# Keys in the heads' channels for two cross-attentions, quotients taken from PSUM, remainders by halves

## What is computed

```python
HEAD_DIM = DIM // NUM_HEADS          # 128 // 16 = 8
Q = (x @ Wq.T).reshape(B, xN, NUM_HEADS, HEAD_DIM)
KV = (z @ Wkv.T).reshape(B, zN, 2, NUM_HEADS, HEAD_DIM)
K = KV[:, :, 0]
V = KV[:, :, 1]
attn = jnp.einsum('bqhd,bkhd->bhqk', Q, K) * SCALE
attn = jax.nn.softmax(attn, axis=-1)
O = jnp.einsum('bhqk,bkhd->bqhd', attn, V).reshape(B, xN, DIM)
return O @ Wo.T
```

## Time and profile before

| | |
|---|---|
| runs | 4034.22, 4035.7, 4037.05 us, median 4035.7 us |
| profiled execution | 4029.83 us, span of the core 4028.0 us |
| busy share of the span | TensorE 94%, VectorE 78%, ScalarE 66%, GpSimd 63% |
| chain that ended last | TensorE 87%, VectorE 6%, GpSimd 2%, ScalarE 2% |
| granted TensorE clock, mean | 0.954 |

### The profile page before, as it was taken

The page is one execution under the profiler, slowest core; times in us unless marked ns, Lnnn a source line. Parts: engine busy times, 40 slices in busy tenths (PEclk is TensorE's granted clock), DMA queues, the critical chain, the costliest instruction groups (busy, mean ns, idle before and its releaser), DMA issues.

```text
span 4028.0 us, 110585 instructions
## 1 busy us (share of the span) xinstructions
PE 3794.2 (94%) x43467; PEld 2887.3 (72%) x43467; DVE 3136.7 (78%) x6499; ACT 2673.5 (66%) x5365; POOL 2545.3 (63%) x2457
## 2 busy tenths in 40 slices
PE   6999999989979999999799999996997899999987
PEld 4777777766647777777577777775665677777765
DVE  6999999858888888887688887886654788888864
ACT  4887887756647777777377777772542577777752
POOL 4888888759856766677466766664001476676761
PEclk8999999979989999999699999997998899999998
DMA  5333333125432221221122122110000212222100
GB/s 130 104 110 111 112 107 109 41 90 159 142 111 57 60 61 54 60 61 43 28 60 61 54 61 61 54 56 19 3 1 18 65 54 64 57 58 63 55 22 15
DMA packets 157328, 266.80 MB, mean 66 GB/s; under 512 B 26632, under 2 KB 97432, under 8 KB 155432
## 3 DMA queue, kind: packets, MB, share of 16 engines
q1 hardware_dynamic: 156360, 259.67, 22.6%
q10 hardware_dynamic: 448, 0.06, 0.0%
HBM read 165.10 MB, written 50.26 MB: 53 GB/s over the span
## 4 chain that ended last, share of the span: by engine, by line
PE 87%; DVE 6%; POOL 2%; ACT 2%; DMA 1%; issue 1%; SPq 1%; POOLq 0%; DVEq 0%; ACTq 0%
PE ps L186 83%; PE ps L665 1%; DVE xn L166 1%; POOL wst L545 1%; PE ps L242 1%; DVE wst L823 1%; PE ps L255 1%; PE ps L1639 1%; DMA big<-big 1%; PE ps L1161 0%; DVE st L151 0%; DVE wst L778 0%; DVE relu L775 0%; ACT wb L324 0%; PE ps L193 0%
## 5 line engine op out<-in xcount | busy, mean ns | idle before, releaser
L545 POOL TENSOR_TENSOR wst<-wst 125x384 bf16<-125x384 f32 (+1 forms) x1536 | 1432.2, 932 | 833.1 <-ACT wst L751 772.3
L751 ACT ACTIVATE wst<-ps 125x448 f32<-125x448 f32 x3072 | 1518.1, 553 | 568.3 <-PE ps L186 553.8
L186 PE MATMUL ps<-big,cx 128*125 128x448 bf16 (+1 forms) x6144 | 1427.4, 353 | 0.7 <-DMA big<-topT 0.7
L186 PEld LDWEIGHTS ps<-cx,wst 125*128 125x128 bf16 x23040 | 1113.6, 98 | 307.5 <-POOL wst L545 15.2
L823 DVE TENSOR_TENSOR wst<-wst 125x512 bf16<-125x512 f32 (+1 forms) x1536 | 1270.2, 827 | 56.7 <-ACT wst L751 56.5
L186 PE MATMUL ps<-cx,wst 125*128 125x65 bf16 (+2 forms) x23040 | 1202.4, 204 | 12.1 <-POOL wst L545 11.6
L186 PEld LDWEIGHTS ps<-big,cx 128*125 128x125 bf16 (+1 forms) x6144 | 834.5, 137 | 283.9 <-issue 1.8
L186 PE MATMUL ps<-cx,big 128*128 128x500 bf16 (+1 forms) x2688 | 709.8, 317 | 10.2 <-DVE big L1744 2.6
L778 DVE TENSOR_REDUCE wst<-ps 128x1 f32<-128x500 f32 x896 | 604.5, 675 | 136.3 <-PE ps L186 123.6
L775 DVE CUSTOM_DVE_ANT_0 wst<-ps,wst 128x500 bf16<-128x500 f32 x448 | 302.9, 676 | 195.0 <-PE ps L186 150.5
L775 DVE CUSTOM_DVE_ANT_0 relu<-ps,relu 128x500 bf16<-128x500 f32 x448 | 302.1, 674 | 149.7 <-PE ps L186 81.4
(11 more groups left out here) (250 smaller groups left out, 4213.2 us busy)
## 6 DMA issues: line engine op xcount, KB each, us to landing
big<-big SPq DMA_DIRECT2D x768, 56.0 KB, 2.7
cx<-ctxT SPq DMA_DIRECT2D x96, 375.0 KB, 3.5
cx<-ctxN SPq DMA_DIRECT2D x64, 377.9 KB
cx<-in_ctxN SPq DMA_DIRECT2D x64, 375.0 KB
cx<-ctxT SPq DMA_DIRECT2D x96, 187.5 KB, 3.8
ctxN<-cx SPq DMA_DIRECT2D x32, 377.9 KB
ynN<-cx SPq DMA_DIRECT2D x32, 377.9 KB
cx<-ynN SPq DMA_DIRECT2D x32, 377.9 KB
```

What stands on the lines that cost most here:

```text
L186: return t.matmul(o, l, r, start=start, stop=stop, skip_group_check=True)
L545: g.tensor_tensor(pl[r][0:KP, at:], pf[r][0:KP, at:], pf[r][0:KP, at:].bitcast(BF16)[:, 1::2], ALU.subtract).then_inc(s["plp"], 1)
L751: e.activation(pf[T % 3][0:KP, cols], bank(2 + n2 % 3, 448)[0:KP], ACT.Exp, scale=scale).then_inc(s["ev"], 1)
```

## The change

In stages 1 and 2 the keys are now projected on the chip into the heads' own channels (16 heads x 8 = 128 rows). Per batch three times two matmuls of 500 columns into bank 7 (`pe_keys`), ScalarE makes the high part `KH` (`act_keys`), VectorE the low part `KL` (`dve_keys`); both are stored to DRAM (`headk`) and loaded back in four groups of four heads, three times 32 rows (high, low, high) and a row of ones (`Ks`). The query is projected once for a pair of batches (three matmuls of 128 columns), stored to DRAM so that it lies block-diagonal there (`headq`), and loaded back as `Qm` (128 x 896, for the maxima) and `Qs` (97 x 896, for the scores). A score half is then two matmuls of 224 columns instead of two of 448. New loops `pe_head`, `act_head`, `dve_head`, `sp_head` hold the schedule of these two stages. The folding of query weights ahead of them falls away; stage 2's bias enters with the query.

In all four stages the values' 129-column matmul is split in 65 and 64, the accumulator has two buffers (`acc`), and a batch's end becomes: reciprocal and quotient on VectorE out of PSUM, rounding on ScalarE, remainder on GpSimd.

The remainder's border is 640, 448, 448, 512 for the four stages. In stages 1 and 2 VectorE's part now waits for the first exponential half alone, and GpSimd's part waits in addition until VectorE's of the same step is done (`s["pl"]`). Eight DMAs that clear `headq` are added at the program's start, ahead of the first context loads.

```diff
-JP = (5, 4, 4, 4)
+SPLIT = (640, 448, 448, 512)
...
+        acc = [bank(5 + i, 65 * NJ) for i in range(2)]
...
+        KH, KL = ([cTs[:, 1500 * v + 750 * i:1500 * v + 750 * i + 750].bitcast(BF16) for i in range(2)] for v in range(2))
+        Ks = [big[:, 3008 * i:3008 * i + 3008].bitcast(BF16).rearrange("p (g n) -> p g n", g=4) for i in range(2)]
+        Qm = [big[:, 6016 + 448 * i:6464 + 448 * i].bitcast(BF16) for i in range(2)]
+        Qs = [big[:, 6912 + 448 * i:7360 + 448 * i].bitcast(BF16) for i in range(3)]
+        kD = nc.dram_tensor("headk", [2, 2, 128, M], BF16).ap()
+        qD = nc.dram_tensor("headq", [4, 2, H * (8 * HQ + NQ)], BF16).ap()
...
+            if f in EARLY:
+                w.wait_ge(s["w"], (0, 224, 336)[f])
+                e.activation(wqh, wqs[:, 0:128], ACT.Copy).then_inc(s["f1a"], 1)
+                e.activation(wkh, wks, ACT.Copy).then_inc(s["f1a"], 1)
+            for j in () if f in EARLY else range(1 if f == 3 else 0, H // per, 2 if f == 3 else 1):
...
-                    r, at = (T - 1) % 3, 128 * JP[ci]
+                    r, at = (T - 1) % 3, SPLIT[ci]
                     w.wait_ge(s["ev"], evacuated(ci, T - 1) + 2)
+                    if ci in (1, 2):
+                        w.wait_ge(s["pl"], NT * ci + T)
                     g.tensor_tensor(pl[r][0:KP, at:], pf[r][0:KP, at:], pf[r][0:KP, at:].bitcast(BF16)[:, 1::2],
                                     ALU.subtract).then_inc(s["plp"], 1)
                     w.wait_ge(s["plp"], NT * ci + T)
-                if 0 <= (k := due(T, KT + 4)) < B - 1:
-                    u, kb = k % 2, B * ci + k
-                    r = raw[u][:, :, 0:C]
-                    w.wait_ge(s["fc"], 2 * (kb + 1))
-                    g.tensor_tensor(r, r, raw[u][:, :, C + 1:], ALU.add).then_inc(s["fp"], 1)
-                    w.wait_ge(s["fp"], 4 * kb + 1)
...
-                if 0 <= (k := due(T, KT + 8)) < B - 1:
-                    u, kb = k % 2, B * ci + k
-                    r = raw[u][:, :, 0:C]
...
-                    g.tensor_copy(O[:, k % HB, :, 0:C], r).then_inc(s["fp"], 1)
-                    w.wait_ge(s["fp"], 4 * kb + 3)
-                if 0 <= (k := due(T, KT + 10)) < B - 1:
-                    u, kb = k % 2, B * ci + k
-                    r = raw[u][:, :, 0:C]
-                    g.tensor_tensor(O[:, k % HB, :, C:], r, O[:, k % HB, :, 0:C], ALU.subtract).then_inc(s["fp"], 1)
-                    w.wait_ge(s["fp"], 4 * kb + 4)
+                if 0 <= (k := due(T, KT + 6)) < B - 1:
+                    kb = B * ci + k
+                    w.wait_ge(s["fp"], 2 * kb + 1)
+                    g.tensor_tensor(O[:, k % HB, :, C:], raw[k % 2], O[:, k % HB, :, 0:C], ALU.subtract).then_inc(s["fp"], 1)
+                    w.wait_ge(s["fp"], 2 * kb + 2)
+
+        def pe_values(t, w, ci, T):
+            k, i = divmod(T, KT)
+            r, kb = T % 3, B * ci + k
+            ph, o, of = pf[r][0:KP, :].bitcast(BF16)[:, 1::2], acc[k % 2], cnb[k % 3]
+            w.wait_ge(s["pl"], NT * ci + T + 1)
+            wait_values(w, ci, k)
+            if kb >= 2:
+                w.wait_ge(s["fc"], kb - 1)
+            for j in range(NJ):
+                if 128 * j == SPLIT[ci] or j == 3 and SPLIT[ci] == 448:
+                    w.wait_ge(s["plp"], NT * ci + T + 1)
+                cols, at = slice(128 * j, 128 * j + 128), 65 * j
+                mm(t, o[:, at:at + 65], ph[:, cols], of[:, i, 0:65], i == 0 and j == 0, False)
+                mm(t, o[:, at:at + 64], ph[:, cols], of[:, i, 65:129], False, False)
+                n = mm(t, o[:, at:at + 65], pl[r][0:KP, cols], of[:, i, 0:65], False, i == KT - 1)
+            n.then_inc(s["pv"], 1)
+
+        def dve_values(v, w, ci, k):
+            u, kb = k % 2, B * ci + k
+            o = acc[u].rearrange("p (j c) -> p j c", j=NJ)
+            w.wait_ge(s["pv"], KT * (kb + 1))
+            v.reciprocal(rden[u][:, :], o[:, :, C]).then_inc(s["rd"], 1)
+            if k >= 2:
+                w.wait_ge(s["fp"], 2 * (kb - 1))
+            w.wait_ge(s["rd"], kb + 1)
+            v.tensor_tensor(raw[u], o[:, :, 0:C], per_row(rden[u][:, :], C), ALU.mult).then_inc(s["fc"], 1)
+            if k == B - 1:
+                w.wait_ge(s["fp"], 2 * kb + 1)
+                v.tensor_tensor(O[:, k % HB, :, C:], raw[u], O[:, k % HB, :, 0:C], ALU.subtract).then_inc(s["fp"], 1)
+
+        def act_values(e, w, ci, k):
+            kb = B * ci + k
+            w.wait_ge(s["fc"], kb + 1)
+            w.wait_ge(s["fp"], 2 * kb)
+            if k >= HB:
+                w.wait_ge(s["otr"], kb - HB + 1)
+            e.activation(O[:, k % HB, :, 0:C], raw[k % 2], ACT.Copy).then_inc(s["fp"], 1)
...
+        KEY_SLOT = {21: (4, 0), 1: (2, 1), 4: (2, 2), 8: (3, 0), 12: (3, 1), 16: (3, 2)}
...
+        def sp_head(y, w, ci):
...
+            for T in range(-44, NT):
+                if (k := due(T, -44)) >= 0:
+                    i = k % 3
+                    if k >= 3:
+                        w.wait_ge(s["pm"], projected(ci, "keys", k - 3, 2))
+                    y.dma_start(cs[i], cT2[k]).then_inc(s[f"lT_{i}"], 16)
+                if (k := due(T, -18)) >= 0:
+                    u = k % 2
+                    w.wait_ge(s["pa"], projected(ci, "keys", k, 2))
+                    if k >= 2:
+                        wait_operands(w, ci, k - 2)
+                    y.dma_start(kD[u, 0], KH[u]).then_inc(s[f"stT_{u}"], 16)
+                    w.wait_ge(s["pd"], projected_low(ci, "keys", k, 2))
+                    y.dma_start(kD[u, 1], KL[u]).then_inc(s[f"stT_{u}"], 16)
+                if (m := 0 if T == -44 else (T + 23) // 24 if (T + 23) % 24 == 0 and T > 0 else NP) < NP:
...
+                    w.wait_ge(s["pa"], projected(ci, "query", m))
+                    for v, of in enumerate((qhb, qlb)):
+                        for r in range(2):
+                            y.dma_start(diagonal(qD[2 * (m % 2) + r, v]), of[m % 2][:, 64 * r:64 * r + NQ]).then_inc(s[f"qd_{m % 2}"], 16)
+                        w.wait_ge(s["pd"], projected_low(ci, "query", m))
+                if (k := 0 if T == -44 else due(T, -22) or -1) >= 0:
+                    wait_query_stored(w, ci, k // 2)
+                    if k >= 2:
+                        w.wait_ge(s["mxm"], products_to(b0 + k - 1, ORDER[0]))
+                    y.dma_start(Qm[k % 2], rows_of(qD[k % 4, 0])).then_inc(s[f"ql_{k % 2}"], 16)
+                if (k := due(T, -14)) >= 0:
+                    if k >= 2:
+                        wait_operands(w, ci, k - 2)
+                    if k >= 3:
...
+                    for n, v in enumerate((0, 0, 1)):
+                        y.dma_start(Qs[k % 3][32 * n:32 * n + 32, :].rearrange("r (g c) -> r g c", g=4),
+                                    grouped(qD[k % 4, v])).then_inc(s[f"lx_{k % 2}"], 16)
+                if (k := due(T, -11)) >= 0:
+                    u = k % 2
+                    wait_keys_stored(w, ci, k)
+                    if k >= 2:
+                        w.wait_ge(s["sc"], 2 * (t0 + KT * (k - 1)))
+                    for n, v in enumerate((0, 1, 0)):
+                        y.dma_start(Ks[u][32 * n:32 * n + 32, :, 0:M], by_group(kD[u, v])).then_inc(s[f"lx_{u}"], 16)
...
+                if (k := due(T, -3)) >= 0:
+                    w.wait_ge(s["ev"], (2 * NT + B) * ci + 2 * max(0, KT * k - 4) + k + 1)
+                    y.dma_start(Qs[k % 3][96:97, :], topT[k % 2][:, :]).then_inc(s[f"tops_{k % 2}"], 16)
+        def pe_keys(t, w, ci, k, c):
+            wait_keys(w, ci, k)
+            o, of = bank(keys_bank(k, c), 500), cs[k % 3][:, 500 * c:500 * c + 500]
+            mm(t, o, wkh, of, True, False)
+            mm(t, o, wkl, of, False, True).then_inc(s["pm"], 1)
...
+                    for hf in range(2):
+                        w.wait_ge(s["ev"], evac + n2 - 2)
+                        for g in (2 * hf, 2 * hf + 1):
+                            at = 4 * NQ * g
+                            r = mm(t, bank(2 + n2 % 3)[:, at - 448 * hf:at - 448 * hf + 4 * NQ],
+                                   Ks[u][0:97, g, KP * i:KP * i + 128], Qs[k % 3][0:97, at:at + 4 * NQ], True, True)
+                        r.then_inc(s["sc"], 1)
+                        n2 += 1
...
+                    w.wait_ge(s["ev"], evacuated(ci, T - 1) + 1)
+                    to = SPLIT[ci]
+                    v.tensor_tensor(pl[r][0:KP, 0:to], pf[r][0:KP, 0:to], pf[r][0:KP, 0:to].bitcast(BF16)[:, 1::2],
+                                    ALU.subtract).then_inc(s["pl"], 1)
+                what, p, c = head_slot(T)
+                if what == "keys split":
+                    dve_keys(v, w, ci, p, c)
+                if what == "query split":
+                    query(p)```

How the change moves instructions, in stage 1. Three places follow. First **TensorE**, one step in the middle of the stage, before (`big,cx` are scores, `cx,wst` values, 128x500 a product for the maxima); the block 129, 65 goes on for seven column blocks:

```

460 lines of the change are left out of this document (342 added, 118 removed).

## The result

The changed kernel takes 4051.45 us (median of 5 runs, 4049.77 to 4056.58) against 4035.7 before; the ratio is 1.0041, 95% interval 1.0026 to 1.0056. It is slower by 16 us, under half a per cent but clear of the noise, where 119 us less were forecast. The profiled execution has a span of 4051.6 us, 23.6 more than before.

What follows compares the result with a forecast made beforehand. TensorE bounded the kernel; afterwards VectorE and GpSimd together would, at 1.78 us a step. Stages 1 and 2 -108, folding -14, stage ends -6, beginnings +6, start +3: -119, so 3916 us, range 3845 to 4005.

Steps and rivals of the forecast that it cites:

- both paths stand in every step, and the longer counts: Stages 1 and 2: port path of 1.56 us or VectorE's own instructions, whichever longer; 42.5 us per 24 steps.
- The slack that I counted on: Stages 1 and 2: three buffers for `pf` were said to give over 1 us of slack against a longer chain.
- The new ones cost nothing: TensorE's values: six of 21 matmuls are new, each with a weight load; columns set the pace, so no added time.
- The small terms: Outside the steps: folding -14, stage ends -6, beginnings of stages 1 and 2 +6, program start +3 us.
- run ahead of the turn: Beginning of stages 1 and 2: three key projections precede the turn, GpSimd's clearing hidden; uncovered, both cost some 2 us.
- Program start: Eight more DMAs ahead of the context loads: between 0 and 13 us, taken as +3.
- the stage ends: End of each of four stages: 2.3 us from copy to turn instead of 3.7, -6 us in all.
- The longer chain: Rival, stages 1 and 2: late reduction stops TensorE through two product banks; 1.85 to 1.90 us a step, 3965 to 4005; chance 0.22.
- The late query: Rival, every pair: TensorE's first product waits for `Qm`, late by 9.7 us, 310 us in all, 4226; chance 0.07.
- The granted clock: Rival: TensorE idles a tenth of the time, clock falls to 1.2 GHz, 1.62 us a step doubles; chance 0.01.
- TensorE as the limit: Rival, stages 1 and 2: GpSimd gets its port without delaying VectorE; 1.62 us a step, 3800 us; chance 0.12.
- The signs: Trace marks: piece returns every 42.7 us, TensorE under 95%, GpSimd's remainder 0.93 minimum, VectorE's over 0.9 in light steps.

Runs made afterwards that it cites:

- e3: Changed kernel with VectorE's remainder put ahead of the step's first reduction in stages 1 and 2: 3924.01 us, ratio 0.9730 to the kernel before.
- e1: Kernel before, with the 129-column value matmul split into 65 and 64 columns in all four stages: 4070.89 us, ratio 1.0098.
- e6: Changed kernel, stages 1 and 2: VectorE's remainder first, GpSimd's cut to 128 columns from the fourth step, the rest left out: 3883.61 us, ratio 0.9620.
- e7: Kernel before, with VectorE's remainder ahead of the step's first reduction in all four stages: 4110.67 us, ratio 1.0191.
- e10: Changed kernel with TensorE issuing the next step's first product ahead of this step's values in stages 1 and 2: 4084.22 us, ratio 1.0122.
- e13: Changed kernel, TensorE order in stages 1 and 2: second product, scores, next first product, values: 4133.85 us, ratio 1.0245 to the kernel before.

## Why the prediction was wrong

**The step that failed: "both paths stand in every step, and the longer counts", with 42.5 us as the outcome.** The two paths were the waits between VectorE and GpSimd. I didn't follow what stands ahead of VectorE's remainder in its own program: a reduction, which waits for a product, which stands on TensorE behind values, which wait for GpSimd. The order rows ahead of the prediction show the reduction in front of the remainder, and the kernel's text shows each of the waits. So I put VectorE's waiting for a product at nothing; it is most of 7.1 us per 24 steps. The sum of parts was right for a machine in which VectorE is never idle. Once the loop is cut, in e3, 24 steps take 42.43 and 42.34 us against 42.5. In the changed kernel they take 46.65, and stages 1 and 2 came out at +5 in place of -108.

**The slack that I counted on.** I held three buffers for `pf` against a longer chain. They give slack to the exponentials. The loop runs through none of them; its bound is that values lag the scores by two steps, so that two steps can't be shorter than one turn. One turn, from the timeline of the changed kernel: 0.93 of GpSimd; from its end at 1401.97 to the key projection 0.44, for the values left; 0.43 for the key projection where there is one; 0.41 from product to reduction; 0.59 and 0.61 for reduction and remainder; 0.17 of handover. Together 3.58, or 1.79 a step, and 1.58 without a key projection. That is under 1.944, so the loop alone doesn't fill the time: quotients, `diff` and key parts on VectorE fall into it in some steps and aren't made up in the others. VectorE's idle time shows where: nearly all of its 7.1 us per 24 steps stands at nine of the 24, ahead of a reduction that waits for its product or for ScalarE's relu, and in the others VectorE goes from one instruction to the next. How much each kind of work adds I haven't separated. That this loop is in the kernel, and that cutting it gives back the forecast pace, is shown; that it makes up all of the 46.65 isn't.

**TensorE.** "The new ones cost nothing" failed: 28 ns a step by the pace, 43 us over 1536 steps, and 38 measured in e1. That is most of the 19 us of stages 0 and 3, where I had put 0: 0.51 of 0.69 us per 24 steps in stage 0, and all of stage 3's. The other terms that I checked held: scores at 95 ns each (0.38 against 0.39 taken), products and key matmuls 0.21. The Trainium skill's 81 ns a pair at 128 columns (TensorE: Matmul & The Clock Gate, Back-to-back issue gap) is not what this stream shows: 21 pairs of 64 and 65 columns in 0.65 us are 31 ns each. My argument against it went too far the other way.

**VectorE and GpSimd.** The parts held: GpSimd's remainder 0.93 (forecast 0.932), the handover 0.17 in stage 1 (0.15 taken), `diff` 872 ns in the changed kernel beside a running GpSimd and 404 in e3 without it. The Trainium skill (SBUF — State Buffer, Who interferes with whom) says that only these two engines share a port and that it is held whole; both numbers agree. But in the changed kernel the port is not what costs: VectorE's remainder takes 682 ns there, and in e3, where it costs, 789.

**The small terms.** They were to give -11, and gave -0.4. Stage 1 to 2 gave -7.5, with the fold gone; forecast -7 - 1.5 + 3 = -5.5. Stage 0 to 1 gave +4.1 in place of -5.5. There I had counted two landings, of 2.7 and 3.5 us, in place of one. The chain has four, the query's store of 1.85 us at 1194.88 and these:

```profile
1173.62 10.12 DMA cx<-ctxT
...
1198.56 6.80 DMA headk<-cTs
...
1206.67 6.69 DMA big<-headq
```

Before, the chain had one trip there, a landing of 5.08 us at 1179.14, and no load of keys. That load takes 10.12 us here, and the key projections that wait for it stand ahead of the turn on TensorE. My sentence that the projections "run ahead of the turn" had the order right and the price at nothing. Program start gave +4.4 against +3, which the traces can't confirm: the start takes 64.4 to 68.1 us in the four traces with the beginning of the kernel before, and 66.0 to 70.7 in the others. Of the stage ends, the last gave -2.0 and stage 2 to 3 +0.6, where I had -1.5 each.

**The rivals.** The longer chain had 0.22 and the right mechanism in words ("a late reduction stops TensorE"), but I put its size at 1.85 to 1.90 a step without working out a loop, and named slack that doesn't exist. The late query decides nothing in the changed kernel: `big<-headq` lands after 6.9 us in the median, not 8.7, and past the beginnings of stages 1 and 2 TensorE waits for it in three places, 1.0 us at most. In e3 and e6 it is part of what holds TensorE. The granted clock stayed at 1.00 in stage 1's middle. TensorE as the limit (3800) needs GpSimd out of the way and the query earlier; e6 comes to 3884. None of my cases joined a loop in stages 1 and 2 with a split that costs 19 us in the two others; together they are the 4051.

**The signs.** Several that I had named came true and prove nothing, because the loop gives them too: TensorE under 95% (91%), GpSimd's remainder at 0.93, most of its starts right after VectorE's end, VectorE's at 0.61 alone. The two that told the cases apart failed: the piece of the earlier trace rows returns every 46.65 us, not 42.7, and VectorE's remainder has a mean of 682 ns, so it seldom stands at the port.

## What to carry to other kernels

When a change adds a wait between two engines, don't stop at the sum of the two: start at the new wait and follow it backwards through every engine's program until you come to the same instruction of an earlier step, add that turn up, and divide by the number of steps it spans. What can be done early should stand ahead of what comes late: here three lines moved on VectorE turned 16 us lost into 109 gained (3924.01 against 4032.65 on the same chip). But that holds only where the early thing is really there early, as e7 shows, and an operation pulled ahead on the producer alone (e10, e13) fills the buffers of a consumer that hasn't moved.

## What the hardware showed that I hadn't expected

- Splitting a matmul of 129 columns into 65 and 64 costs about 4.7 ns (28 ns for six), little beside a row of the timeline, and 38 us over 1536 steps in e1.
- A wait can be dear and useful in the same kernel: the handover costs 75 us with the reduction first (4051 against 3977) and saves 42 with the remainder first (3924 against 3966).
- The same 375 KB load of keys (`cx<-ctxT`) took 3.5 us to land before and 9.9 in the median after, at 135 GB/s in stage 1 against 58 before. In the chain it stands only at stage 1's beginning.
